# A decoder of four layers on one core: self-attention value products packed and divided, last experts' sums on TensorE

## Time and profile before

| | value |
|---|---|
| median of 3 runs | 4092.17 us (4089.69 to 4092.91) |
| profiled execution | 4104.95 us |
| its span, first to last instruction | 4103.1 us |
| instructions | 91932 |
| PE busy | 3225.7 us (79%), 33262 matmul records |
| DVE busy | 2729.5 us (67%) |
| ACT busy | 2072.7 us (51%) |
| POOL busy | 1254.2 us (31%) |
| granted clock of TensorE, mean | 0.87 |

### The profile page before, as it was taken

The page is one execution under the profiler, slowest core; times in us unless marked ns, Lnnn a source line. Parts: engine busy times, 40 slices in busy tenths (PEclk is TensorE's granted clock), DMA queues, the critical chain, the costliest instruction groups (busy, mean ns, idle before and its releaser), DMA issues.

```text
span 4103.1 us, 91932 instructions
## 1 busy us (share of the span) xinstructions
PE 3225.7 (79%) x33262; PEld 2229.8 (54%) x33262; DVE 2729.5 (67%) x7583; ACT 2072.7 (51%) x4651; POOL 1254.2 (31%) x2347
## 2 busy tenths in 40 slices
PE   6886888696888676967898989677883579879884
PEld 2443555473556455854555555344553456669884
DVE  5884767364778576547787878476766468865455
ACT  2664656322444453535787878453660234345563
POOL 2321222102121234451111111243322424534666
PEclk9987999697999787977999999687995599989997
DMA  5423332032221322231212121423412260122323
GB/s 92 69 38 55 59 54 39 21 100 40 37 39 18 57 60 66 85 72 38 47 30 45 29 43 31 59 39 60 60 32 71 72 112 21 50 85 85 94 75 92
DMA packets 322828, 232.76 MB, mean 57 GB/s; under 512 B 53901, under 2 KB 305531, under 8 KB 322199
## 3 DMA queue, kind: packets, MB, share of 16 engines
q1 hardware_dynamic: 308106, 198.55, 24.7%
q0 software_dynamic: 13408, 27.54, 2.2%
q10 hardware_dynamic: 864, 0.79, 0.1%
HBM read 69.28 MB, written 55.75 MB: 30 GB/s over the span
## 4 chain that ended last, share of the span: by engine, by line
PE 26%; DVE 13%; POOL 7%; issue 6%; ACT 4%; DMA 2%; SPq 1%; DVEq 0%; ACTq 0%; POOLq 0%
PE ps L1505 4%; PE ps L1314 3%; PE ps L3939 2%; PE ps L3948 2%; PE ps L1348 2%; POOL PT L3763 2%; PE ps L727 2%; PE ps L1452 2%; ACT PT L1412 1%; DVE M L1362 1%; POOL L_sorted_results L3751 1%; PE ps L1126 1%; DVE X L406 1%; DMA SKB<-MT 1%; DVE BS L378 1%
## 5 line engine op out<-in xcount | busy, mean ns | idle before, releaser
L1412 ACT ACTIVATE PT<-ps 128x512 f32<-128x512 f32 (+1 forms) x1600 | 812.0, 560 | 339.6 <-PE ps L1348 247.4
L1362 DVE TENSOR_REDUCE M<-ps 128x2 f32<-128x512 f32 x1024 | 652.6, 683 | 128.6 <-PE ps L1348 103.8
L1314 PE MATMUL ps<-SKB 51*128 51x256 bf16 (+3 forms) x3584 | 414.4, 276 | 115.7 <-DVE M L1362 66.2
L1359 DVE TENSOR_REDUCE M<-ps 128x3 f32<-128x384 f32 x768 | 390.6, 550 | 150.5 <-PE ps L1348 92.7
L1505 PE MATMUL ps<-PT,VA 128*9 128x256 f32 (+1 forms) x7168 | 455.7, 374 | 1.4 <-ACT PT L1412 1.2
L4021 ACT ACTIVATE SKB<-ps,SKB 128x128 f32<-128x128 f32 x1032 | 295.1, 370 | 242.4 <-PE ps L3939 241.0
L1452 PE MATMUL ps<-SKB 53*128 53x256 bf16 (+3 forms) x3584 | 357.8, 268 | 47.2 <-DMA SKB<-MT 37.3
L1348 PE MATMUL ps<-tri,idh 64*128 64x128 bf16 x5120 | 392.9, 222 | 0.0
L4091 DVE COPY SKB<-SKB 128x1028 f32 (+1 forms) x258 | 185.7, 720 | 259.7 <-PE ps L3948 232.4
L1314 PEld LDWEIGHTS ps<-SKB 51*128 51x128 bf16 (+1 forms) x3584 | 131.2, 96 | 385.9 <-DVE M L1362 158.1
L3948 PE MATMUL ps<-SKB 128*128 128x128 f32 x2064 | 286.6, 284 | 28.4 <-ACT SKB L4021 28.3
(11 more groups left out here) (520 smaller groups left out, 6403.3 us busy)
## 6 DMA issues: line engine op xcount, KB each, us to landing
SKB<-HH SPq DMA_DIRECT2D x1212, 64.0 KB
SKB<-HH SPq DMA_DIRECT2D x576, 32.0 KB
L_sorted_results<-SKB SPq DMA_DIRECT2D x195, 64.0 KB
PT<-L_sorted_rows SPq DMA_DIRECT2D x150, 64.0 KB
SKB<-in_L3f_w SPq DMA_DIRECT2D x32, 256.0 KB, 3.6
L_sorted_rows<-TV SPq DMA_DIRECT2D x2, 4032.0 KB, 32.4
SKB<-scratch SPq DMA_DIRECT2D x2, 2048.0 KB, 11.5
SKB<-in_L1f_w SPq DMA_DIRECT2D x16, 256.0 KB, 3.2
```

What stands on the lines that cost most here:

```text
L1314: k = e.matmul(self.mx_bank(m + i)[:, o:o + n], K.QS[self.set(c)][64 * i:64 * i + rows, s, 256 * bb + 128 * qt:256 * bb + 128 * qt + 128], ...
L1359: k = e.tensor_reduce(K.M3[n % 2][:, hh, 0:3], mx[:, 0:384].rearrange("p (a k) -> p a k", a=3), axis=AX.X, op=ALU.max)
L1362: k = e.tensor_reduce(K.M3[n % 2][:, hh, 0:2], mx.rearrange("p (a k) -> p a k", a=2), axis=AX.X, op=ALU.max)
L1412: e.activation(K.PT[:, x % 4, n * i:n * i + n], self.st_bank(x, i)[:, 0:n], ACT.Exp, bias=0.0, scale=self.scale).then_inc(*self.exp.inc())
```

## The change

For the self attentions: VA becomes two buffers with 27 columns for a pair of heads (values and one; nine zeros; values and one), so that a product with 18 columns adds one head into its own 9 rows and zeros to the other 9. Heads of j = 0, 1 and of j = 2, 3 then accumulate in the same 18 rows of a row group, and the bank is copied, turned and normalised once a unit instead of twice. The products of j = 0, 1, 2 are divided by key tile: the first tile (8 records) stays in slot LE + 2j + 3, the second goes to the slot after, between `pe_max` and `pe_exp`. With three repetitions ("quick") VectorE still normalises, from PSUM, with one reciprocal and four multiplications a unit. In the other four attentions ScalarE copies bank 7 to VN, VectorE takes reciprocals of VN and GpSimd does the four multiplications (two for the cross part). The negated maxima take two instructions instead of four. The values are projected later, and the slots of turning, output and stacking move (OOS, OUT, TURN, V, KP, KSTK).

For the last experts: the roots of chunks 0 to 4 move from GpSimd to VectorE (`dve_root`), and the sums of chunks 5 to 7 are made by TensorE in PSUM (`pe_results`: an identity times x and times each of the four results); VectorE takes moments and scales from there. Index changes of M3 to MX3, the step argument of `newton`, the same layout in `dve_values`, the source argument of `dve_moments` and `dve_norm`, and `pool_normalise_cross` (two products of 128 elements) are left out below.

```diff
-        self.VA = [sb(f"VA{i}", [128, 64, 9]) for i in range(3)]
+        self.VA = [sb(f"VA{i}", [128, 32, 27]) for i in range(2)]
...
+        self.MX3 = [t[:, :, :].rearrange("p a b -> p (a b)").rearrange("p (q h) -> p q h", q=4) for t in self.M3]
...
+        self.OV = sb("OC", [128, 288])
+        self.OC = self.OV[:, 0:256].rearrange("p (a b) -> p a b", a=2)
...
-            e.memset(v[:, :, 8:9], 1.0)
+            e.memset(v[:, :, 8:27:18], 1.0)
+            e.memset(v[:, :, 9:18], 0.0)
...
+    def dve_root(self, e, c):
         K, n = self.K, self.norm(c)
-        rr = self.rows(c)
+        e.wait_ge(*self.seed.at(n))
+        newton(e, K.dv, K.NW[n % 2], K.RSD[n % 2][:, 0:4]).then_inc(*self.root.inc())
...
+        m, mb = K.MX3[n % 2], K.MB[n % 2]
         if n >= 2:
             e.wait_ge(*self.mbt.at(n - 2))
+        if order == "self":
+            v = m[:, 0:2, :].rearrange("p q h -> p (q h)").rearrange("p (x b) -> p x b", b=8)
+            o = mb[:, :, :].rearrange("p q r -> p (q r)").rearrange("p (x s b) -> p x s b", s=2, b=8)
+            e.wait_ge(*K.dv.now())
+            e.tensor_scalar(o[:, :, 0, :], v, -1.0, None, ALU.mult).then_inc(*K.dv.inc())
+            e.wait_ge(*K.dv.now())
+            e.scalar_tensor_tensor(out=o[:, :, 1, :], in0=v, scalar=-1.0, in1=o[:, :, 0, :], op0=ALU.mult, op1=ALU.subtract
+                                   ).then_inc(*self.negmax.inc())
+            return
...
+    def act_vn(self, e, f):
+
+        K = self.K
         e.wait_ge(*self.tvt.at(f))
-        e.reciprocal(r, v[:, :, :, 8:9]).then_inc(*K.dv.inc())
+        if f > 0:
+            e.wait_ge(*self.nrm.at(f - 1))
+        e.activation(self.VN, K.PS[:, 7, :].rearrange("p (x k) -> p x k", k=32)[:, :, 0:18], ACT.Copy, bias=0.0, scale=1.0
+                     ).then_inc(*self.vn.inc())
...
+        sums = K.PS[:, 7, :].rearrange("p (x k) -> p x k", k=32)[:, :, 8:18:9]
+        e.reciprocal(K.RC[f % 2][:, 0:32].rearrange("p (x e) -> p x e", e=2), sums).then_inc(*K.dv.inc())
         e.wait_ge(*K.dv.now())
-        v = K.PS[:, 7, :].rearrange("p (q b h k) -> p q b h k", q=2, b=4, h=2)
-        r = K.RC[f % 2][:, 0:16].rearrange("p (q b h o) -> p q b h o", q=2, b=4, o=1)
+        for h in range(2):
+            for half in range(2):
+                k = e.tensor_tensor(out[:, :, h, 4 * half:4 * half + 4, :], v[:, :, :, h, 9 * half:9 * half + 8],
+                                    r[:, :, :, h, half:half + 1].to_broadcast([128, 2, 4, 8]), ALU.mult)
+        return k
+
+    def dve_recip(self, e, f):
+        K = self.K
+        e.wait_ge(*self.vn.at(f))
+        sums = self.VN.rearrange("p x (e k) -> p x e k", e=2)[:, :, :, 8]
+        e.reciprocal(K.RC[f % 2][:, 0:32].rearrange("p (x e) -> p x e", e=2), sums).then_inc(*self.rc.inc())
+
+    def pool_normalise(self, e, f, oo):
+
+        K = self.K
+        v = self.VN.rearrange("p (q b h) (e k) -> p q b h e k", q=2, h=2, e=2)
+        r = K.RC[f % 2][:, 0:32].rearrange("p (q b h e) -> p q b h e", q=2, h=2, e=2)
         out = oo.rearrange("p q (h d b) -> p q h b d", h=2, d=8)
-        for par in range(2):
-            k = e.tensor_tensor(out[:, :, par, 4 * half:4 * half + 4, :], v[:, :, :, par, 0:8],
-                                r[:, :, :, par, :].to_broadcast([128, 2, 4, 8]), ALU.mult)
+        e.wait_ge(*self.rc.at(f))
+        for h in range(2):
+            for half in range(2):
+                k = e.tensor_tensor(out[:, :, h, 4 * half:4 * half + 4, :], v[:, :, :, h, half, 0:8],
+                                    r[:, :, :, h, half:half + 1].to_broadcast([128, 2, 4, 8]), ALU.mult)
+        return k
+
...
-    LE, MBT, CMBT, TV, GATE = 12, 9, 11, (5, 9, 11), 8
+    LE, MBT, CMBT, GATE = 12, 9, 11, 8
+    TV = (9, 11)
...
-        self.OOS = LE + (14 if cross else 12 if gate else 11)
-        self.OUT, self.TURN = self.OOS + 1, 6 if cross or gate else 5
-
-        self.Q, self.KP, self.V = (-30, -20, -13) if cross else (-29, -20, -19) if rope else (-29, -27, -19) if gate else (-25, -15, -19)
-        self.QSTK, self.KSTK = (-26, -17) if cross else (-20, -12) if reps > 1 else (-14, -20) if gate else (-20, -14)
+        self.quick = reps > 1
+        self.OOS = LE + (15 if cross else 11 if self.quick else 14)
+        self.OUT, self.TURN = (28, 5) if cross else (31, 8) if gate else (31, 6) if rope else (24, 4)
+
+        self.Q, self.KP, self.V = (-30, -20, 6) if cross else (-29, -20, -1) if rope else (-29, -27, 8) if gate else (-24, -13, 2)
+        self.QSTK, self.KSTK = (-26, -17) if cross else (-20, -11) if reps > 1 else (-14, -20) if gate else (-20, -14)
...
-        self.plan(units, start, L, start[-1] + self.OUT + 12)
+        self.plan(units, start, L, start[-1] + max(36 + gate + 3 * cross, self.OUT + (9 if kind == "keep" else self.TURN) + 2))
...
-        self.nf, self.nm = 2 + cross, 1 + cross
+        self.nf, self.nm = 1 + cross, 1 + cross
...
+        self.VN = (K.GG[:, 0:288] if cross or gate or reps > 1 else K.OV[:, :]).rearrange("p (x k) -> p x k", k=18)
+        self.vn, self.rc = (K.ev(name, 0 if self.quick else nu * self.nf) for name in ("values_out", "value_recips"))
...
-        if c >= 3:
-            e.wait_ge(*self.pv.at(self.np * self.last[c - 3] + 3))
+        if c >= 2:
+            e.wait_ge(*self.pv.at(self.np * self.last[c - 2] + 3))
...
-        e.activation(K.VA[self.set(c)][:, :, 0:8], K.PS[:, 7, :].rearrange("p (a k) -> p a k", k=8), ACT.Copy, bias=0.0,
-                     scale=1.0).then_inc(*self.vact.inc())
+        v = K.PS[:, 7, :].rearrange("p (x e b k) -> p x e b k", e=2, b=4, k=8)
+        va = K.VA[c % 2][:, :, :].rearrange("p (x b) k -> p x b k", b=4)
+        for half in range(2):
+            k = e.activation(va[:, :, :, 18 * half:18 * half + 8], v[:, :, half, :, :], ACT.Copy, bias=0.0, scale=1.0)
+        k.then_inc(*self.vact.inc())
...
-    def pe_pv(self, e, u, j):
+    def pe_pv(self, e, u, j, tiles):
         K = self.K
         c, bb = self.units[u][0] // 2, self.units[u][0] % 2
-        f = self.nf * u + j // 2
+        f = self.nf * u
         x = self.nx * u + 2 * j
-        if j % 2 == 0 and f > 0:
+        if j == 0 and f > 0 and 0 in tiles:
             e.wait_ge(*self.tv.at(f - 1))
-        if j == 0 and bb == 0 and self.units[u][1] == 0:
+        if j == 0 and bb == 0 and 0 in tiles and self.units[u][1] == 0:
             e.wait_ge(*(self.vact if self.W["vb"] is None else self.vdve).at(c))
-        e.wait_ge(*self.exp_done(x + 1))
-        g = j % 2
-        for kt in range(2):
+        if 0 in tiles:
+            e.wait_ge(*self.exp_done(x + 1))
+        g, half = j % 2, j // 2
+        for kt in tiles:
             for i in range(4):
                 lo = 128 if kt == 1 and self.causal else 0
                 o = 256 if kt == 1 else 0
                 pt = K.PT[:, (x + i // 2) % 4, 0:2 * self.width].rearrange("p (a k) -> p a k", a=2)
-                k = e.matmul(K.PS[32 * i:32 * i + 9, 6, 256 * g + lo:256 * g + 256],
-                             K.VA[self.set(c)][:, (2 * bb + kt) * 16 + 8 * (i % 2) + 2 * j + i // 2, :], pt[:, i % 2, o:o + 256 - lo],
-                             start=kt == 0, stop=kt == 1)
-        k.then_inc(*self.pv.inc())
+                pair = (2 * bb + kt) * 8 + 4 * (i % 2) + 2 * g + i // 2
+                k = e.matmul(K.PS[32 * i:32 * i + 18, 6, 256 * g + lo:256 * g + 256],
+                             K.VA[c % 2][:, pair, 9 * half:9 * half + 18], pt[:, i % 2, o:o + 256 - lo],
+                             start=j == 0 and kt == 0, stop=j == 3 and kt == 1)
+        if 1 in tiles:
+            k.then_inc(*self.pv.inc())
...
+        for j in range(3):
+            u = self.at(g, LE + 2 * j + 4)
+            if u is not None:
+                self.pe_pv(e, u, j, (1,))
...
-                self.pe_pv(e, u, j)
+                self.pe_pv(e, u, j, (0,) if j < 3 else (0, 1))
...
-        for h, off in ((0, LE + 6), (1, LE + 10), (2, LE + 12)):
-            u = self.at(g, off)
+        for h, off in enumerate(self.TV):
+            u = self.at(g, LE + off + 1)
             if u is not None and h < self.nf:
-                self.pe_tvt(e, self.nf * u + h, self.nrm.at(self.nf * u + h))
+                self.pe_tvt(e, self.nf * u + h, (self.nrm if self.quick else self.vn).at(self.nf * u + h))
...
-        for h, off in ((0, LE + 5), (1, LE + 9), (2, LE + 11)):
-            u = self.at(g, off)
+        for h, off in enumerate(self.TV):
+            u = self.at(g, LE + off)
             if u is not None and h < self.nf:
-                f = self.nf * u + h
-                self.act_tv(e, f, self.pv.at(self.np * u + 2 * h + 1))
+                self.act_tv(e, self.nf * u + h, self.pv.at(self.np * u + 2 * h + 3))
...
+        for h, off in enumerate(self.TV):
+            u = self.at(g, LE + off + 1)
+            if u is not None and h < self.nf and not self.quick:
+                self.act_vn(e, self.nf * u + h)
...
+        for h, off in enumerate(self.TV):
```

(47 more changed lines are left out.)

116 lines of the change are left out of this document (65 added, 51 removed).

## The result

The changed kernel takes 4112.98 us (4102.32 to 4128.87), the kernel before 4091.64 us on the same chip: a ratio of 1.0053, interval 1.0042 to 1.0065. It is 0.5% slower; the forecast was 2.5% faster. The profiled execution has a span of 4104.3 us and 90427 instructions, against 4103.1 and 91932. So I read periods and stages from the traces, and whole times from the ratios.

A forecast was written before the change was run, and what follows sets the result against it. It took TensorE and VectorE alternating, neither full alone, to bound the attentions. Terms -14.6 (turning and dividing), -76.6, +4, -10.5 and -3 sum to -100.7 us: 3991.5 us for the median, range 3955 to 4035, chance 0.63.

The forecast's parts named there:

- Turning once: Self attentions: one of each unit's two turns goes, taking 0.76 us of TensorE off a unit.
- Dividing: Self attentions: each of three value products split into two blocks of 8 adds 0.21 us, 0.63 a unit, on TensorE.
- The rival that wider products cost more: Value products with 18 rows cost 19 ns more a record, +136 us, giving 4127 us; chance 0.07.
- The waits: Ahead of the maxima matmuls (L1314): 80% of TensorE's 95.8 us waiting for VectorE's reductions goes, -76.6 us.
- the waits only move: Rival: uneven slots keep TensorE and VectorE alternating, so only blocks, roots, last sums and queue count, 4068 us; chance 0.13.
- TensorE waits at L1452: Sign that the forecast is wrong: TensorE waits at the exponent scores, or ahead of the second tile, instead; no size.
- The queue of SyncE: Three repetitions: K stacked one slot later crowds its 12 DMAs before the maxima's DMA, +4 us, bounds 0 and +15.
- To GpSimd: In 64 units, normalisation products move from VectorE to GpSimd, about 1.3 us a unit there, covered by later slots.
- rival 4074: Each product moved to GpSimd keeps VectorE from running, so 83 us come back, 4074 us; chance 0.03.
- Transitions: Between attention stages: a longer end chain against V's projection leaving the gap, taken as 0, bounds -10 and +10 us.
- The roots: Last experts: three of five roots leave GpSimd's unbroken run of DMAs for VectorE, -10.5 us.
- The last sums: End of the kernel: sums of the last chunks on TensorE take 20.9 us after arrival instead of 24.1, -3 us.

The follow-up runs named there:

- undivided: The changed kernel with both key tiles of every value product in one slot, as in the kernel before; 4071.72 us, ratio 0.9947.
- k_early: The changed kernel with the repeated attention's Q and K projections and K's stacking put back to their earlier slots; 4107.33 us, ratio 1.0033.
- experts_only: The kernel before with only the last experts' part: roots on VectorE, sums of chunks 5 to 7 on TensorE; 4083.83 us, ratio 0.9981.

## Why the prediction was wrong

**Turning once**, -0.76 us a unit: right as work (0.83), wrong as time. The turn stood in light slots, in which TensorE waits: 1.44 us with the turn, 1.29 with the wait. The unit fell by 0.21 (undivided). I had both rows, 2111.26 to 2112.70 and 2108.90 to 2109.51, and didn't set them against each other.

**Dividing**, +0.21 for each of three products: right. Two blocks of 8 take 0.56 us each and 0.10 ahead of each, one of 16 takes 0.99 and 0.10: +0.23, or 0.69 a unit. From undivided to changed TensorE's own time grew by 0.94, most of the other 0.25 around the turn of OO (0.73 us after the block before it where 0.56 is usual, since it waits for VectorE). So as a whole it went from 11.80 to 11.91 us (forecast -0.13). The Trainium skill, "TensorE: Matmul & The Clock Gate", section "Back-to-back issue gap", gives the isolated gap between matmuls from the moving columns; the trace agrees in that the stationary width made no difference (0.99 and 0.98 us for 16 records with 18 and 9 rows). The rival that wider products cost more gave nearly the right time by a mechanism that isn't there.

**The waits**, -76.6 us: this is the step that failed. I counted the waits for VectorE and treated them as the only ones. The forecast said that "the slot that had only scores, in which TensorE waited, now has 0.64 us of work between its maxima and its exponent scores". That is true and is the fault: for the maxima the halves lie in two intervals, for the exponent scores in one. The waits moved from L1314 to L1514. This is a form of the rival "the waits only move" (4068) and of the sign given for being wrong, "TensorE waits at L1452". By that rival a unit would take 13.08 - 0.13 = 12.95 us; it takes 13.47, 0.28 more in waits (three stalls, 1.56 us, against two, 1.28) and 0.24 more in TensorE's own work than forecast. In the other attentions the waits for VectorE, 50.6 of the 95.8 us, were to go too, and 44.2 of them stayed (55.9 with L857); no run says why. And at the changes of chunk of the repeated attention 17.8 us came on top, of which 10.6 went away in k_early: that belongs to the next term.

**The queue of SyncE**, +4 us, bounds 0 and +15: the mechanism right as far as the traces show it, the size low. Putting the three numbers back gave 0.2% or 8 us in the changed kernel (10.6 in the stage), and 26 us where the halves are even. The term counted the DMA's wait alone; what it left out is the stretch at a granted clock of 0.50 behind such a wait.

**To GpSimd**, 0 (rival 4074): VectorE normalising again in the rotary stages changed nothing (1.0058 and 1.0053). The Trainium skill, "SBUF — State Buffer", section "Who interferes with whom", says that tensor_reduce never contends with GpSimd, and the trace agrees: in the two rotary stages of the changed kernel a reduction that runs beside one of GpSimd's products takes 0.68 us (causal 0.56) on average, one with GpSimd idle 0.69 (0.55).

**Transitions**, 0 with bounds of 10 either way: +11.5 us, just beyond the bound. What I also left out is that V, the output projection and x's turn moved within the steady state. In the causal rotary stage that cost 2 us in each pair of units, given back in its last units; the stage with bias gained 15.6 us in all, divided or not (14.8 undivided; 9.2 against experts_only), though no run separates why.

**The value buffers**, 0: not tested by themselves.

**The roots**, -10.5 us: right. Between the DMAs of 3937 and 4066 the changed kernel gains 11.8 us.

**The last sums**, -3 us: right (2.8). TensorE and VectorE after, and two windows:
```profile
4079.98 6.22 PE L3888 MATMUL ps<-XT,idf 128*128 128x512 f32 x8 [14.35 <-DMA XT<-L_sorted_results]
4086.05 1.02 PE L3884 MATMUL ps<-X,idf 128*128 128x512 f32 x2
...
4090.34 1.02 PE L3884 MATMUL ps<-X,idf 128*128 128x512 f32 x2
```
```profile
4100.20 1.37 DVE L414 TENSOR_SCALAR X<-ps,MV,RSD 128x128 f32<-128x128 f32 x4 [2.11 <-POOL RSD L510]
```
```profile
4078.00:4082.00 4.00, 2.02 (x3) 1.01 (x4) 0.00 (x0) 0.00 (x0) 0.00 (x0) 0.50 1.02 360
4086.00:4090.00 4.00, 4.00 (x11) 1.80 (x10) 1.78 (x11) 0.00 (x0) 1.18 (x6) 1.00 0.68 204
```
From arrival to the last scaling's start it is 20.2 us, 23.0 before. After 14 us of idling TensorE starts at a granted clock of 0.50, 1.2 GHz: four products take 6.1 us (forecast 5.4), later ones 0.86 each.

In sum, by ratios: the experts' part -8 to -20 us, the three numbers around K's stacking +8, the division 43, and the remaining changes of the attentions gain less than the division costs. The division alone is the difference between 0.5% faster and 0.5% slower.

## What to carry over

When TensorE feeds two engines through two rings of buffers, a block has to be placed against both: measure the distances of the writes to each ring, not the length of the slots. A wait that the profile shows can hide another behind it that is as long; look for the shortest distance at which the second ring has ever run. And work taken out of a slot in which the engine waits is not time: price it against the wait in that same slot.

## What the runs showed of the hardware

- A block of 8 f32 records costs 0.56 us, one of 16 0.99 (0.98 with 9 rows instead of 18), so a division costs some 0.13 us and another gap of 0.10.
- The exponent scores of two slots never came closer than 1.18 to 1.19 us with three banks in the repeated attention: 0.54 until the first exponential starts, 0.60 for that exponential of 512 elements, 0.05 until the next scores start. With exponentials of 256 elements it is 0.98, with 0.38 in place of 0.60.
- SyncE issued 12 stacking DMAs in 8.4 to 9.7 us, and a DMA placed right behind them was late by 0.5 to 1.8 us. After TensorE's waits of 2.9 to 5.6 us for it, windows of 4 us showed granted clocks of 0.50 to 0.69. Shifting three slot numbers moved the time by 26 us in one kernel and by 8 in another.
- The 23 reductions from PSUM that ran beside GpSimd's products took 0.68 us (causal 0.56), those with GpSimd idle 0.69 (0.55).
